# GNN layer and mixture of experts on one Trainium2 core: router logits as 24 more columns of the node products

## The reference, cut to what matters

```python
def _layernorm(x): ...                      # (x - mean) / sqrt(var + 1e-5)

def gnn(x, dst, src, W, b):
    agg = jnp.zeros_like(x).at[dst].set(x[src])      # one of the sources of each node, or zero
    return jnp.concatenate((x, agg), axis=-1) @ W.T + b

def moe(tokens, router_w, w1, b1, w2, b2):
    probs = jax.nn.softmax(tokens @ router_w.T, axis=-1)
    rw, re = jax.lax.top_k(probs, 2)
    rw = rw / rw.sum(-1, keepdims=True)
    out = tokens
    for e in range(8):
        y = jax.nn.gelu(tokens @ w1[e] + b1[e], approximate=False) @ w2[e] + b2[e]
        out = out + combine[:, e:e + 1] * y          # combine: rw at the two chosen experts, else 0
    return out

x = x + gnn(_layernorm(x), dst, src, W, b)
x = x + moe(_layernorm(x), ...)
```

## Time and profile before

| what | value |
|---|---|
| median of 3 runs | 1196.66 us |
| lowest and highest of them | 1186.67 and 1199.59 us |
| span of the profiled execution | 1180.7 us |
| PE, DVE, ACT, POOL busy in it | 836.3, 868.3, 630.4, 484.9 us |

### The profile page before, as it was taken

One profiled execution on the slowest core, in us unless ns is written; L12 is line 12 of the kernel. 1 busy time (PEld: TensorE's weight loads), 2 busy tenths in 40 slices (PEclk: granted clock), 3 DMA queues, 4 the chain that ended last, 5 costly groups with the idle time before them and its releaser, 6 DMA issues.

```text
span 1180.7 us, 28647 instructions
## 1 busy us (share of the span) xinstructions
PE 836.3 (71%) x9319; PEld 702.9 (60%) x9319; DVE 868.3 (74%) x1893; ACT 630.4 (53%) x1669; POOL 484.9 (41%) x527
## 2 busy tenths in 40 slices
PE   1599888887666862243444468888888888888886
PEld 1588887776555651132333256776766666767766
DVE  6999999995677764477688946776667666766666
ACT  3466666663444331264553345666666565666665
POOL 7000000004445556764650035555555555555554
PEclk9799999999888795555555789999999999999999
DMA  8800000003664444553551712222222222222220
GB/s 228 266 28 27 27 27 27 27 27 84 208 202 149 118 121 144 156 165 99 160 170 63 7 42 68 64 65 61 65 66 64 64 65 66 63 67 65 70 60 11
DMA packets 79211, 104.89 MB, mean 89 GB/s; under 512 B 22593, under 2 KB 64538, under 8 KB 78994
## 3 DMA queue, kind: packets, MB, share of 16 engines
q0 software_dynamic: 21408, 54.87, 16.6%
q1 hardware_dynamic: 57714, 48.76, 14.8%
HBM read 63.16 MB, written 44.01 MB: 91 GB/s over the span
## 4 chain that ended last, share of the span: by engine, by line
PE 31%; DVE 28%; issue 14%; another core or an unknown queue 12%; ACT 8%; DMA 3%; POOL 1%; ACTq 1%; DVEq 1%; SPq 1%; POOLq 0%
PE bank L983 12%; PE bank L997 9%; DVE arena L1099 7%; PE bank L786 6%; DVE arena L1082 5%; ACT arena L750 2%; PE bank L951 2%; PE bank L809 1%; ACT arena L711 1%; DVE bst L1300 1%; DVE arena L1283 1%; DVE big L1297 1%; POOL arena L517 1%; ACT arena L695 1%
## 5 line engine op out<-in xcount | busy, mean ns | idle before, releaser
L983 PE MATMUL bank<-arena,w1s 128*128 128x128 f16 x3000 | 211.2, 220 | 78.0 <-issue 69.1
L983 PEld LDWEIGHTS bank<-arena,w1s 128*128 x3000 | 177.8, 98 | 112.8 <-issue 109.8
L505 POOL DMA_INDIRECT arena<-key_rows,cid x98 | 94.8, 968 | 330.0 <-DVEq L1215 252.7
L750 ACT ACTIVATE arena<-bank,b1s 128x128 f32<-128x128 f32 x500 | 142.0, 368 | 155.6 <-remote 152.1
L532 POOL DMA_INDIRECT out<-arena,gidx x125 | 140.3, 1123 | 188.9 <-DVE arena L1438 149.5
L997 PE MATMUL bank<-w2s,arena 128*128 x1500 | 184.1, 272 | 1.4 <-DVE arena L1418 0.7
L521 POOL DMA_INDIRECT arena<-tok_rows,gidx x125 | 124.4, 995 | 107.4 <-DVE gidx L1407 69.4
L809 PE MATMUL bank<-wgs,arena 128*128 128x256 f16 x1176 | 160.0, 289 | 5.6 <-issue 5.4
L1433 DVE SCALAR_TENSOR_TENSOR arena<-bank,arena 128x256 f32<-128x256 f32 x125 | 60.1, 481 | 132.7 <-remote 129.5
L997 PEld LDWEIGHTS bank<-w2s,arena 128*128 128x128 f16 x1500 | 140.7, 98 | 17.8 <-issue 1.7
L809 PEld LDWEIGHTS bank<-wgs,arena 128*128 128x128 f16 x1176 | 121.7, 104 | 34.1 <-issue 8.6
(11 more groups left out here) (215 smaller groups left out, 1414.9 us busy)
## 6 DMA issues: line engine op xcount, KB each, us to landing
agg_rows<-arena SPq DMA_DIRECT2D x49, 256.0 KB
tok_rows<-arena SPq DMA_DIRECT2D x13, 896.0 KB
big<-x SPq DMA_DIRECT2D x5, 1792.0 KB, 14.1
arena<-w SPq DMA_DIRECT2D x16, 256.0 KB, 2.9
big<-x SPq DMA_DIRECT2D x6, 512.0 KB
arena<-tok_rows,gidx POOLq DMA_INDIRECT x125
out<-arena,gidx POOLq DMA_INDIRECT x125
arena<-key_rows,cid POOLq DMA_INDIRECT x98
```

The source lines that it names most:

```text
L505: gp.indirect_dma_start(er[:, b % 2, s, :], None, key_rows, bass.IndirectOffsetOnAxis(cid[:, t:t + 1], 0)).then_inc(er_full[b % 2], 16)
L750: last = sc.activation(h32[:, u % 2, at:at + P], bank[2 + u % 2][:, at:at + P], ACT.Gelu, bias=b1s[:, ds(e[x], 1), f], scale=1.0 / SCALE)
L983: last = mm(bank[2 + u % 2][:, at:at + P], parts[x, w, c, f], a[:, u % 4, c * P:(c + 1) * P], start=(n == 0), stop=(n == 5))
```

## The change

**The router in the node products.** A logit is the row after both layers' normalisation times a column of `router_w`. It is linear in x, in the own part of the product and in the gathered part, so it can be put together from three products of 8 columns with the normalised node row: with W_x times the router's weights, with the router's weights themselves (which give x, by the row's mean and deviation), and with W_agg times the router's weights. These 24 columns are composed once at the start: `compose()`, 12 small f32 products on PE from two new inputs (W in another order, 0.5 MB, and the bias as a column), copied and split by ACT and DVE. `node_linear` has 12 more products of 24 columns a pair; they go to the first 48 columns of bank 0 or 1, which are the banks that the transposes of every second pair overwrite, and so `node_transposes` waits for `agg_copied` of the pair two before (new). `take_products` makes three copies in place of one. `agg_rows` has rows of 264 floats in place of 256.

**The neighbour stage without PE.** `turn`, `logit`, `copy_transposed` and `low_turned` are gone. `row_logits` (a reciprocal and five operations over 98 x 8 elements) stands before the first addition; each addition adds 8 columns of the gathered rows too. The logits are not yet normalised: `route` subtracts the mean times the sum of the router's column (two more operations), and the difference of the two largest is multiplied by the reciprocal deviation at the end.

**The additions in two parts**, tiles 0 to 3 and 4 to 6 of a piece, with a semaphore for each part of a buffer.

**Five routings** in place of four: 28, 28, 28, 6 and 8 tiles, after pieces 4, 8, 11, 12 and at the end. They wait for `t_ready` (ACT's L711).

The removed functions `turn`, `logit`, `copy_transposed` and `low_turned` are left out here, with the layout of SBUF.

```diff
+XC = 3 * E
+AROW = D + E
...
-ROUTED = [(n, min(RG, T - n)) for n in range(0, T, RG)]
+ROUTED = [(0, 28), (28, 28), (56, 28), (84, 6), (90, 8)]
...
+HALF = 4
...
+def halves_of(n):
+    more = PIECES[n][1]
+    return [(0, min(HALF, more)), (HALF, more)][:2 if more > HALF else 1]
+
+
+def gathered(n, h):
+    return 16 * sum(b - a for k in range(n % 2, n + 1, 2) for a, b in halves_of(k)[h:h + 1])
 
...
+    agg_rows = nc.dram_tensor("agg_rows", [NP + P, AROW], f32).ap()
...
+        bank01 = psum("bank01", 2)
+        bank = [bank01[:, 0:512], bank01[:, 512:1024]] + [psum(f"bank{i}", 1)[:, :] for i in range(2, 8)]
+        extra = bank01[:, :].rearrange("p (k n) -> p k n", k=2)[:, :, 0:2 * XC].rearrange("p k (h n) -> p k h n", h=2)
...
+            sp.dma_start(bcols[:, :], bcol).then_inc(s_small, 16)
+            sp.dma_start(wnf.rearrange("p a b -> p (a b)"), wn).then_inc(s_wn, 16)
...
-            sp.wait_ge(s_small, 48)
+            sp.wait_ge(s_small, 64)
+            sp.wait_ge(row_padded, 1)
             sp.dma_start(agg_rows[NP:NP + P, :], bgs[:, :]).then_inc(s_brow, 16)
...
                     gp.indirect_dma_start(pg[:, n % 2, s, :], None, agg_rows,
-                                          bass.IndirectOffsetOnAxis(gat[:, t:t + 1], 0)).then_inc(pg_full[n % 2], 16)
+                                          bass.IndirectOffsetOnAxis(gat[:, t:t + 1], 0)
+                                          ).then_inc(pg_full[n % 2][s // HALF], 16)
...
                 act.wait_ge(g_ready, i + 1)
                 if not first:
                     act.wait_ge(agg_stored[k], 8 * (i - k))
-                sc.activation(pb[:, k, :], bank[5 + k][:, :], ACT.Copy, scale=1.0 / SCALE).then_inc(agg_copied, 1)
+                sc.activation(pb[:, k, :, 0:D], bank[5 + k].rearrange("p (h d) -> p h d", h=2), ACT.Copy, scale=1.0 / SCALE)
+                sc.activation(pb[:, k, :, D:AROW], extra[:, k, :, 2 * E:3 * E], ACT.Copy, scale=1.0 / SCALE)
+                sc.activation(lx[:, ds(2 * i, 2), :], extra[:, k, :, 0:2 * E], ACT.Copy, scale=1.0 / SCALE
+                              ).then_inc(agg_copied, 1)
...
             adid.settle()
             root(1)
-            before_pairs = adid.n
             act.wait_ge(s_wg, 16)
             sc.activation(wgs[:, 0, :, :].rearrange("p a b -> p (a b)"), wgf, ACT.Copy, scale=SCALE).then_inc(linear_high, 1)
+            act.wait_ge(composed, 1)
+            parts = bank[7][:, 0:4 * E].rearrange("p (s c e) -> p s c e", s=2, c=2)
+            sc.activation(wxf[:, :, 0:E], parts[:, 0, :, :], ACT.Copy, scale=SCALE)
+            sc.activation(wxf[:, :, 2 * E:3 * E], parts[:, 1, :, :], ACT.Copy, scale=SCALE)
+            sc.activation(rowk[:, :, :].rearrange("p a e -> p (a e)"), bank[7][:, 4 * E:6 * E], ACT.Copy)
+            adid.done(sc.activation(wxf[:, :, E:2 * E], rws[:, :, :], ACT.Copy, scale=SCALE))
+            before_pairs = adid.n
+            adid.settle()
+            sc.activation(wxs[:, 0, :, :], wxf[:, :, :], ACT.Copy).then_inc(wx_high, 1)
             act.wait_ge(s_brows, 48)
...
             pe.wait_ge(consts_ready, 7)
+
+            def compose():
+                pe.wait_ge(s_small, 64)
+                pe.wait_ge(s_wn, 16)
+                pe.wait_ge(row_padded, 2)
+                for q in range(4):
+                    for o in range(2):
+                        mm(bank[7][:, q * E:(q + 1) * E], wnf[:, o, q * P:(q + 1) * P], rws[:, o, :],
+                           start=(o == 0), stop=(o == 1))
+                for o in range(2):
+                    mm(bank[7][:, 4 * E:5 * E], one32[:, :].broadcast_to([P, P]), rws[:, o, :], start=(o == 0), stop=(o == 1))
+                for o in range(2):
+                    last = mm(bank[7][:, 5 * E:6 * E], bcols[:, o:o + 1].broadcast_to([P, P]), rws[:, o, :],
+                              start=(o == 0), stop=(o == 1))
+                last.then_inc(composed, 1)
...
+                    n = 0
+                    for c in range(2):
+                        for a, w in ((xh, 0), (xh, 1), (xl, 0)):
+                            last = mm(extra[:, k, h, :], a[:, k, h * D + c * P:h * D + (c + 1) * P], wxs[:, w, c, :],
+                                      start=(n == 0), stop=(n == 5))
+                            n += 1
                 last.then_inc(g_ready, 1)
 
             def node_transposes(i, k, first):
                 pe.wait_ge(xn_ready, 2 * i + 2)
                 if not first:
                     pe.wait_ge(xl_ready, i - 1)
+                    pe.wait_ge(agg_copied, i - 1)
...
+            compose()
             pe_pair(0, 0)
             pe.wait_ge(s_brows, 48)
+            pe.wait_ge(wx_high, 1)
...
+                dve.wait_ge(wx_high, 1)
+                ve.tensor_tensor(wxs[:, 1, :, :], wxf[:, :, :], wxs[:, 0, :, :], ALU.subtract)
                 dve.wait_ge(s_wg, 16)
                 dve.wait_ge(linear_high, 2)
...
-                logit = bank[LBANK[c]][:, 0:n * E].rearrange("p (t e) -> p t e", e=E)
+                logit = us[:, of, :]
                 lg, oh = lgc[:, 0:n, :], ohc[:, 0:n, :]
                 a, b, u, v, w = (x[:, 0:n] for x in (av, bv, uu, vv, ww))
+                step(ve.tensor_tensor(oh, mv[:, of, 0:1].broadcast_to([P, n, E]),
+                                      rowk[:, 0, :].unsqueeze(1).broadcast_to([P, n, E]), ALU.mult))
+                step(ve.tensor_tensor(logit, logit, oh, ALU.subtract))
                 step(ve.tensor_reduce(mx[:, of], logit, AX.X, ALU.max))
...
+            def row_logits():
+                every = [P, T, E]
+                srw = rowk[:, 0:1, :].broadcast_to(every)
+                dve.wait_ge(agg_copied, T // 2)
+                ve.reciprocal(std[:, :], rstd[:, :])
+                step(ve.tensor_tensor(us, nmr[:, :].unsqueeze(2).broadcast_to(every), srw, ALU.mult))
+                step(ve.tensor_tensor(us, lx[:, :, E:2 * E], us, ALU.subtract))
+                step(ve.tensor_tensor(us, us, std[:, :].unsqueeze(2).broadcast_to(every), ALU.mult))
+                step(ve.tensor_tensor(us, us, lx[:, :, 0:E], ALU.add))
+                step(ve.tensor_tensor(us, us, rowk[:, 1:2, :].broadcast_to(every), ALU.add))
+
+            row_logits()
             dve.wait_ge(self_added, T // 2 - IB)
             for n, (first, more) in enumerate(PIECES):
                 of = slice(first, first + more)
-                dve.wait_ge(pg_full[n % 2], gathered(n))
-                step(ve.tensor_tensor(xs[:, of, :], xs[:, of, :], pg[:, n % 2, 0:more, :], ALU.add))
-                dve.sem_inc(pg_used, 1)
-                for s in range(more):
-                    last = ve.bn_stats(bst3[:, s, :], xs[:, first + s, :])
-                step(last)
+                for h, (a, b) in enumerate(halves_of(n)):
+                    rows = slice(first + a, first + b)
+                    dve.wait_ge(pg_full[n % 2][h], gathered(n, h))
+                    ve.tensor_tensor(us[:, rows, :], us[:, rows, :], pg[:, n % 2, a:b, D:AROW], ALU.add)
+                    step(ve.tensor_tensor(xs[:, rows, :], xs[:, rows, :], pg[:, n % 2, a:b, 0:D], ALU.add))
+                    if b == more:
+                        dve.sem_inc(pg_used, 1)
+                    for s in range(a, b):
+                        last = ve.bn_stats(bst3[:, s, :], xs[:, first + s, :])
+                    did.done(last)
+                did.settle()
                 for s in range(more):
                     last = ve.bn_aggr(mv[:, first + s, :], bst3[:, s, :])
                 step(last)
                 dve.sem_inc(var_ready, 1)
-                if n >= 1:
-                    low_turned(turned(first) - 1)
                 dve.wait_ge(std_ready, T // 2 + n + 1)
                 step(ve.reciprocal(rstd[:, of], std[:, of]))
                 ve.scalar_tensor_tensor(nmr[:, of], mv[:, of, 0], -1.0, rstd[:, of], ALU.mult, ALU.mult
                                         ).then_inc(ln_ready, 1)
-                if n == 5 or n == 9:
-                    route(n // 4 - 1)
-                if n == len(PIECES) - 3:
-                    low_turned(turned(first))
-                    route(2)
-
-            low_turned(len(TURNED))
+                if n in (4, 8, 11, 12):
+                    dve.wait_ge(t_ready, 70 if n > 8 else 7 * (n - 1))
+                    route((4, 8, 11, 12).index(n))
+
...
-            route(3)
+            dve.wait_ge(t_ready, T)
+            route(4)
+            step(ve.tensor_tensor(m2, m2, rstd[:, :], ALU.mult))
```

139 lines of the change are left out of this document (36 added, 103 removed).

## The result

The changed kernel takes 1203.6 us (median of 22 runs, 1197.68 to 1211.69) against 1191.18 us (22 runs, 1186.66 to 1201.03): a ratio of 1.0095, 95% interval 1.0074 to 1.0115. That is 1% slower. (A ratio is taken over fast runs alone, without those over 1.5% above the fastest of their kernel, so it is not quite the quotient of the two medians.) The prediction had 1186 us, 0.9% under the median it was made against: the time lies in its range of 1158 to 1228, and the sign is wrong. Later series of runs found more: there are two conditions in which both kernels run.

A forecast was written before the change was run, and what follows sets the result against it. DVE bounds the edge stage, waits for signals the node and neighbour stages. Start +1.5, node stage +22 and neighbour stage -34 sum to -10.5 us: span 1170.2, plus 16 us from span to median, 1186 us; range 1158 to 1228.

The forecast's parts named there:

- Start and edge stage: Start: composition and two more DMAs cost +1.5 us, bounds 0 and +5; edge stage: 0 us.
- its cover: Edge stage: PE's extra 0.35 us per step hides in its 1.07 us wait for DVE; without it, 8 us.
- I take it that this signal is held to the end of the gathers: Node stage: the late transposes' signal, 3 to 6 us into the gathers, reaches ACT only at their end; 21 us.
- The term of 22 us: Node stage: loss from the transposes' new wait and two more ACT copies, +22 us with the last pairs.
- Rival 2: Node stage: PE at half clock, its products also held until the gathers end; total 1222 us; chance 0.28.
- the tail: Neighbour stage's end: DVE 9.4 us behind the last landing, then the last rows and routing; done at 609, against 643.8 before.
- the ring: Neighbour stage: gather, addition, transposition and subtraction take the 194 us; after the change POOL is the bound, done at 591.
- A routing of 28 tiles ... fits in between after pieces 4 and 8: Neighbour stage: DVE needs 6.4 us a piece against POOL's 9.6, so these routings fit in between.
- the cost of the additions in two parts: Neighbour stage: gathers starting within an addition are lengthened, 0.85 us a piece, 12 us for 14 pieces.
- Nothing waits for PE: Neighbour stage: with PE's work gone there, no engine waits for its signals and POOL becomes the bound.
- The 28 us that the prediction worked out from the rule: Neighbour stage: two additions stop POOL for their full 2.03 us a piece, 28 us; the prediction kept 12.
- The third rival: Neighbour stage: nothing won, as rows land later with longer gathers and DVE's tail grows; 1195 to 1210 us; chance 0.05.

The follow-up runs named there:

- n8: The kernel before with nothing but the additions in two parts: 1203.03 us, 1.0134 of before.
- n11: The kernel before, unchanged, profiled once more, with prompt signals: 999.32 us.
- n7: The changed kernel with additions in one part and without the 12 products, the two small copies and the new wait (leaves work out): 1159.25 us.
- n6: The changed kernel with extra columns in banks 4 and 7, no new node-stage wait, one-part additions, without the two small ACT copies (leaves work out): 1173.16 us.
- n5: The changed kernel with the node stage's extra columns in banks 4 and 7 without the new wait, and additions in one part: 1179.12 us, 0.9924 of before.
- n2: The changed kernel without the 12 products and the two small copies, but with the new wait (leaves work out): 1171.84 us, 0.9867 of before.
- a3: The changed kernel with own banks, one-part additions and the 12 products behind the transposes two pairs on, held signals: 1179.54 us, 0.9957 of before.
- a1: The changed kernel, unaltered, run and profiled once more with held signals: 1199.57 us, 1.0159 of before.
- n4: The changed kernel with each piece added in one part of seven tiles: 1192.9 us, 1.0039 of before.

## Why the prediction was right or wrong

**Start and edge stage: right, the start in part by luck.** +1.5 us in the first profile and between -0.6 and +1.5 in the others with the composition. Without it the first key gather starts at 276.6 (n8), 277.3 and 278.0 us (n11), so a term of 1.5 can't be told from the spread. In the window of 28 to 272 us DVE is busy 235.5 us against 236.5 in the earlier trace rows, while PE has 11 us more work: its cover held.

**Node stage: the mechanism right, the size not.** The step "I take it that this signal is held to the end of the gathers" is what the rows at 402.65 and 408.92 show. The term of 22 us measured 37.8. What failed is its split: I put the loss on the wait and the copies, and let the 12 products count only inside the time between release and signal. n7, n6, n5 and the changed kernel give 177.2, 194.3, 197.5 and 213.1 us: products 17 where they were put at nothing, copies 3 as forecast, wait 16 (10 where it is alone, n2 against n7). The products are some 0.6 us a pair (six take 0.30), but they stand ahead of the next transposes on PE, and those had little margin: by the semaphore times in the traces of before, n7 and n6, signals of PE up to 1.5 us into seven key gathers came within 0.01 us (one in n6 after 0.6), one at 1.9 and one at 2.2 came only behind their end, and of those more than 2.4 us in none came at once. In n7 the transposes end 1.25 us in. It is no sharp border: in a3 two signals at 3.7 us in came within 0.01 us. Rival 2, a serial chain with held products, was bounded at 58 to 90 us and wasn't it: from the third on the cycles are 13.9 to 18.7 us, none 22.

**Neighbour stage: the tail right, the ring wrong.** "DVE's tail" behind the last gather went from 69.4 to 57.3 us, -12.1, where the prediction's numbers (644 - 615.7 and 609 - 591) give -10. The gathers were to go from 163.1 to 138.4 us and took 155.4. Two steps failed. "A routing of 28 tiles ... fits in between after pieces 4 and 8" was put at nothing, by DVE's busy time alone; POOL stood 24.8 us in its two long stops (in a1 three of 3.9, 4.8 and 9.9 us). The drawn-out routing of 13.2 us makes most of the second; the first has a routing of 6.0 and some 17 us of DVE's waits around the statistics and the root (6.1, 1.6, 6.8, 1.5 and 0.9). The other is the cost of the additions in two parts, 12 us, with 4 us for the other operations: POOL's gathers were lengthened by 6 us in all, not 16; this term was too high. The prediction's 1.2 us a piece for one addition is what n4 has (16 us in 14 pieces), while the kernel before, whose gathers often stand, had 102.6 - 92.7 = 9.9 us. The stage is DVE's and POOL's alone, and I took held signals to be PE's trouble ("Nothing waits for PE"). In the changed kernel they hit DVE's waits for its own results and for ACT's root.

With one part a gather that begins in an addition of 2.02 us takes 1.98, and the gathers are lengthened by 16 us in all (109.2 - 98 x 0.948). The Trainium skill (SBUF — State Buffer, "SBUF: two separate sides") has the two engines exclude each other there, whoever starts first. The trace agrees in one direction only: the gather begun inside the addition waits, but a gather that is already running is not lengthened, and neither is the addition that begins beside it (2.02 us at 546.28 in n4). The 28 us that the prediction worked out from the rule did not come, with one part or two.

**The sum.** Forecast: +1.5 + 22 - 34 = -10.5 us. Measured: +1.5 + 37.8 - 19.9 = +19.4. Every term has the right sign, and two that are off by 15 us each turn the sum's. Both of the prediction's signs of being wrong came: the neighbour stage won less than 25 us and the node stage lost more than 35. With the second profile of the changed kernel (a1) the sum is +0.9 + 37.7 - 27.1 = +11.5, nearer to the medians; the 7 us between the two are how the gathers fell. The third rival (nothing won, 1195 to 1210 us) names the measured time, but not the reason: 20 to 27 us were won in the neighbour stage, and the node stage gave them back. That span and median lie 16 us apart did not carry over either: the changed kernel has 1203.9 and 1203.6.

**With prompt signals** the prediction's sign is right, and so almost is its size: the spans differ by 988.0 - 997.6 = -9.6 us. That is luck, as the forecast rests on held signals and each term measures half or less of it: +8.5 for 22, -17.1 for -34.

## What to carry to other kernels

With held signals 12 products of 0.6 us together cost 17 us over the 13 cycles, 1.3 us in each; with prompt signals they cost nothing. Look for the signal that just makes it before a burst of gathers, and measure its margin, before you cost an addition at its own length. Putting the extra columns into a bank that was in use made a new wait, and two free banks took it away. And compare side by side, in more than one series: the same two kernels were 1% apart in opposite directions in two conditions that the kernel doesn't choose, so an edit that is good in both (own banks and one part: 0.992, 0.994 and 0.991) is worth more than one that wins in one.

## What the runs showed of the hardware that I had not expected

- One kernel, one input: 1191 us in four series, 1000 us in two, at granted clocks of 0.880 and 0.890 and with equal durations of the single operations, but for the token gathers. The difference is waits that the profile calls "remote" or "issue". What decides it is not settled; one chip ran in both conditions.
- With held signals even DVE's wait for its own last operation takes 1.0 us longer, in steps of 0.7 us (starts 1.40 and 0.70 us apart at 600.99 to 609.39), and goes on for a few operations after the last gather's end (617.68 - 9.63 = 608.05). With prompt signals no routing of 28 tiles took over 6.2 us.
- Fewer collisions went with a slower kernel. With held signals two parts cut POOL's lengthened time from 16 to 6 us, and the changed kernel was 10.7 us slower by the medians (0.6% by the ratios); the kernel before was 12.6 us slower. Why is open.
